# First graph layer of the last four spans by running sums over gathered rows, with those spans built first and as counts only

## What is computed

```python
x1 = x
for l in range(3):                      # GRU layers, float32
    m   = x1 @ weight[l]
    agg = segment_sum(m[src] * edge_weight[:, None], dst, 6250)
    x1  = gru_cell(agg, x1, w_ih, w_hh, b_ih, b_hh)   # r, z sigmoid; n tanh; blend
x = layernorm(x + x1)
x2 = x
for W, b in ((W0, b0), (W1, b1), (W2, b2)):           # count layers
    x2 = relu((x2 + segment_sum(x2[src], dst, 6250)) @ W.T + b)
out = layernorm(x + x2)
```

## Time and profile before

| | us |
|---|---|
| median of 3 runs | 2880.29 (2880.04 to 2880.68) |
| the profiled execution | 2883.43 |
| its span in the profile | 2881.7 |
| PE busy | 2832.6 |
| DVE, ACT, POOL busy | 1246.0, 947.4, 872.5 |
| line 1247, aggregate of the first layer, PE busy | 570.2 |
| line 1240, the build, PE busy | 346.5 |
| line 969, second and third layer, PE busy | 888.4 |
| line 1165, count layers, PE busy | 780.6 |

### The profile page before, as it was taken

The page is one execution under the profiler, slowest core; times in us unless marked ns, Lnnn a source line. Parts: engine busy times, 40 slices in busy tenths (PEclk is TensorE's granted clock), DMA queues, the critical chain, the costliest instruction groups (busy, mean ns, idle before and its releaser), DMA issues.

```text
span 2881.7 us, 72532 instructions
## 1 busy us (share of the span) xinstructions
PE 2832.6 (98%) x29387; PEld 1881.3 (65%) x29387; DVE 1246.0 (43%) x2716; ACT 947.4 (33%) x1891; POOL 872.5 (30%) x1007
## 2 busy tenths in 40 slices
PE   6999999999999999999999999999999999999998
PEld 5899999999999955555555555555655555555554
DVE  7678877777888514344422344343500010001011
ACT  6777777777777610000001011101400010001111
POOL 4344344443444315554541454544000000000000
PEclk7999999999999999999999999999999999999999
DMA  5666666666662398998996988988487868886884
GB/s 196 267 262 244 245 261 261 257 241 251 262 263 95 113 397 342 350 339 326 355 369 253 340 338 331 357 330 327 149 326 301 310 248 301 309 304 247 318 304 163
DMA packets 134009, 810.64 MB, mean 281 GB/s; under 512 B 17208, under 2 KB 27308, under 8 KB 113948
## 3 DMA queue, kind: packets, MB, share of 16 engines
q1 hardware_dynamic: 111228, 758.32, 67.9%
q0 software_dynamic: 19968, 40.46, 4.4%
q10 hardware_dynamic: 2720, 10.62, 0.9%
HBM read 553.01 MB, written 256.33 MB: 281 GB/s over the span
## 4 chain that ended last, share of the span: by engine, by line
PE 95%; issue 2%; DVE 1%; ACT 1%; DMA 1%; another core or an unknown queue 0%; POOL 0%; DVEq 0%; SPq 0%; ACTq 0%; POOLq 0%
PE ps L969 29%; PE ps L1165 27%; PE ps L1247 19%; PE ps L1240 11%; PE ps L979 1%; PE ps L980 1%; PE ps L1260 1%; PE ps L1261 1%; PE ps L982 1%; PE ps L981 1%; PE ps L1144 1%; ACT ring L1661 0%; DMA sum_rows<-ring 0%; PE ps L1266 0%; PE ps L1267 0%
## 5 line engine op out<-in xcount | busy, mean ns | idle before, releaser
L969 PE MATMUL ps<-ring,Y 128*128 128x448 f32 x2352 | 888.4, 539 | 0.0
L1165 PE MATMUL ps<-ring,Y 128*128 128x448 f16 x4116 | 780.6, 352 | 0.0
L1661 ACT ACTIVATE ring<-ps 128x490 f16<-128x490 f32 (+1 forms) x1344 | 698.3, 651 | 176.7 <-PE ps L1240 169.1
L969 PEld LDWEIGHTS ps<-ring,Y 128*128 128x128 f32 x2352 | 446.4, 190 | 434.8 <-issue 434.8
L1165 PEld LDWEIGHTS ps<-ring,Y 128*128 128x128 f16 x4116 | 402.7, 98 | 373.8
L863 POOL DMA_INDIRECT ring<-y_rows,ring x448 | 431.4, 963 | 518.9 <-PE ps L969 257.7
L1247 PE MATMUL ps<-ring,Y 128*128 (+1 forms) x2744 | 570.2, 360 | 0.4 <-ACT shared L1620 0.4
L1247 PEld LDWEIGHTS ps<-ring,Y 128*128 128x128 f32 x2744 | 503.6, 190 | 8.4 <-ACT shared L1620 0.8
L1240 PEld LDWEIGHTS ps<-shared 64*128 64x128 bf16 x18816 | 320.4, 93 | 76.6 <-issue 59.3
L1240 PE MATMUL ps<-shared 64*128 64x49 bf16 (+1 forms) x18816 | 346.5, 189 | 20.0 <-issue 9.6
L1824 DVE TENSOR_SCALAR ring<-ring 128x128 f32<-128x128 f32 x446 | 130.9, 294 | 388.7 <-DMA ring<-y_rows,ring 205.0
(11 more groups left out here) (196 smaller groups left out, 1450.6 us busy)
## 6 DMA issues: line engine op xcount, KB each, us to landing
ring<-adj_w SPq DMA_DIRECT2D x72, 2688.0 KB
ring<-adj_h SPq DMA_DIRECT2D x42, 2800.0 KB, 9.4
ring<-adj_h SPq DMA_DIRECT2D x42, 2688.0 KB, 9.2
adj_w<-ring SPq DMA_DIRECT2D x48, 2016.0 KB, 11.9
adj_h<-ring SPq DMA_DIRECT2D x56, 1372.0 KB, 5.4
ring<-adj_w SPq DMA_DIRECT2D x24, 2912.0 KB
adj_w<-ring SPq DMA_DIRECT2D x48, 728.0 KB, 6.8
sum_rows<-ring SPq DMA_DIRECT2D x62, 448.0 KB
```

The lines of the kernel that those rows point to most:

```text
L969: mm = pe.matmul(ps[:, bank, 0:GW], Y[:, h, :], slab(s)[:, :, h - h0, :], start=(h == 0), stop=(last and h == TILES - 1))
L1165: mm = pe.matmul(ps[:, par, 0:GW], part[:, h, :], counts_slab(par, s)[:, :, h - h0, :], start=(h == 0 and part is Y_high), stop=(h == TILE ...
L1661: act.activation(strip[:, :, c0:c0 + UNIT * WIN].rearrange("p h (d j) -> p d h j", d=WIN)[:, :, :, w0:w1], psum_unit(a)[:, :, kind, :, :]. ...
```

## The change

The build goes through the spans in another order, `ORDER`: the last four first, then the other 24. The last four are built as counts only: DVE makes two of the three one-hot instructions, PE does one product for each pair and node instead of three, ACT evicts each unit once, POOL makes two casts instead of seven steps, SP stores the counts alone, and no tiles of these spans are added. Their first layer is done by running sums as in the other two layers: the list of edges is loaded at the start, POOL gathers 224 rounds of rows of `x` during the build of the 20 spans in slots 5 to 24 (`RUN_SLOTS`), 11 rounds in a slot and 12 in every fourth, each placed at a half batch of its own (`ROW_POINTS`); ACT scales a round two batches after its gather and DVE adds it four batches after; SP stores four rounds at a time. Two of the rounds stand inside and ahead of `make_columns`. The ends are placed on DVE ahead of slot 25, fetched by POOL in slots 26 and 27, and the four spans' gates follow the last tiles, with `add_tiles` of the last span cut into six parts around them (`TAIL_TILES`); the gates of span 23 come last. The turns of the inputs (`TURNS`) move from batches 4 to 14 to batches 12 to 22.

In all three layers the rows are now summed in place: 16 buffers (`RUN_BUFS`) take the place of 10 and 14, a gather waits for the store of the round 16 before it, and the last two stores of the second and third layer are POOL's (`LAST_STORES`). The loops of DVE, ACT, POOL and SP over the spans are written out; PE keeps its loop. Weights and lists move to other places in SBUF, and the space for POOL's DMA descriptors is set to 8192.

```diff
-ROW_BUFS = 10
-STORE = 7
+RUN_BUFS = 16
+STORE = 4
+FIRST_RUN = GATHERS - RUN_SPANS
+ORDER = [*range(FIRST_RUN, GATHERS), *range(FIRST_RUN)]
+GATE_ORDER = [*range(FIRST_RUN - 1), *range(FIRST_RUN, GATHERS), FIRST_RUN - 1]
+RUN_SLOTS = range(RUN_SPANS + 1, GATHERS - 3)
+ROW_POINTS = [1, 2, 3, 4, 5, 7, 8, 9, 11, 12, 15]
+MORE_POINTS, MORE_EVERY = [14], 4
+LAST_STORES = 2
+SCALE_LAG, SUM_LAG, STORE_LAG = 2, 4, 5
+PLACE_SLOT, ENDS_SLOT = 25, 26
+TAIL_TILES = [0, 6, 15, 24, 33, 42, TILES]
...
+            def fetch_round(turn, i):
+                if i >= RUN_BUFS:
+                    if i % STORE == 0:
+                        use, q = divmod(i // STORE - STORE_TURNS, STORE_TURNS)
+                        pool.wait_ge(s_stored[q], stored_by(turn, q) + 16 * (use + 1))
+                    pool.wait_ge(s_acc, RUN * turn + i - RUN_BUFS + 2)
+                pool.indirect_dma_start(out=run_bufs[:, i % RUN_BUFS, :], out_offset=None, in_=y_rows if turn else x,
...
+            def fetch_at(t, points):
+                for point in points:
+                    i, (k, half) = round_at(t, point), divmod(point, 2)
+                    if i is None:
+                        continue
+                    if half:
+                        pool.wait_ge(s_bev, evicted(t, k) + 1)
+                    else:
+                        pool.wait_ge(s_bmm, UNITS * (BUFS + BATCHES * t + k))
+                    pool.sem_inc(s_mark_pool, 1)
...
+                    fetch_round(0, i)
+
+            def prepare_span(t):
+                par = t % 2
+                n = BATCHES * t
+                fetch_at(t, range(0, 4))
...
+                add_own(t + 1, 1 - par)
+                fetch_at(t, range(4, 6))
+                take_places(t + 2, par)
+                if t in (ENDS_SLOT, ENDS_SLOT + 1):
+                    first = RUN_SPANS // 2 * (t - ENDS_SLOT)
+                    fetch_ends(0, range(first, first + RUN_SPANS // 2))
+                for d, (k, later) in enumerate(zip(FETCH_AT, FETCH_AT[1:] + (6,))):
+                    pool.wait_ge(s_bmm, UNITS * (BUFS + n + k))
+                    pool.sem_inc(s_mark_pool, 1)
+                    gather(par, d)
+                    fetch_at(t, range(2 * k + 1, 2 * later))
+                make_columns(t + 1, 1 - par, t)
+                fetch_at(t, [14])
+                near_rows(t + 3, 1 - par)
+                fetch_at(t, [15])
...
                 for kind in range(2):
                     col_step(pool.tensor_copy(columns[:, par, :, kind, :, :], batches(kind).to_broadcast([P, BATCHES, BATCH, 2])))
+                fetch_at(slot, [12, 13])
                 rest = batches(2)
-                for p in range(WPARTS):
+                for p in range(WPARTS if has_weights(t) else 0):
...
+            def scale_rows(n):
+                for i in rounds_at(n):
+                    row = run_bufs[:, i % RUN_BUFS, :]
+                    act.wait_ge(s_row[i % RUN_BUFS], 16 * (i // RUN_BUFS + 1))
+                    act.activation(row, row, ACT.Copy, scale=run_edges[:, i, 1:2]).then_inc(s_prod if i else s_acc, 1)
...
+            def sum_row(turn, i):
+                done = RUN * turn + i
+                row, last = (run_bufs[:, j % RUN_BUFS, :] for j in (i, i - 1))
+                dve.wait_ge(s_acc, done)
+                dve.wait_ge(s_prod, done - turn)
+                dve.scalar_tensor_tensor(out=row, in0=last, scalar=run_edges[:, i, 2:3], in1=row,
+                                         op0=ALU.mult, op1=ALU.add).then_inc(s_acc, 1)
...
+            for c, n in enumerate(range(FIRST_RUN - 2, GATHERS)):
+                add_tiles(0, TAIL_TILES[c], TAIL_TILES[c + 1])
+                if n < GATHERS - 1:
+                    fused_gates(n)
...
+                if c < RUN_SPANS:
+                    flip_run(c)
```

## The result

| | before | after |
|---|---|---|
| median, us | 2880.53 (6 runs) | 2983.39 (2977.91 to 3021.43, 6 runs) |
| profiled execution, its span | 2883.43, 2881.7 | 2982.35, 2980.6 |

After stands to before as 1.0384 (95% interval 1.0348 to 1.042): **103 us slower**, where 2830 us was forecast.

A forecast was written before the change was run, and what follows sets the result against it. PE alone was taken to bound the steady build, busy for all 820.80 us. The terms -136.8 + 70.0 - 9 + 13.2 + 12 + 0 = -50.6 on a span of 2881.7 gave 2831.1, so 2830 us, range 2806 to 2868.

The forecast's parts named there:

- Part 5: Rows in the 20 spans: PE waits 0.6 us for columns in each, +12 us; lower end 0, upper end +116.
- Part 4: Behind the steady spans: four spans' gates 9.2 us, flips 2, placing ends 2, gathers of ends nothing; +13.2 us.
- the tail: Work behind the steady spans: four spans' gates at 9.2 us and flips at 2 us, within Part 4.
- Part 1: Steady build: four spans fewer that cost PE its full time, 4 x 34.2 = -136.8 us.
- Part 2: Four spans of counts at 17.5 us each, +70.0 us; bounds 15.5 and 25.7 us a span.
- Part 3: The start: first one-hot sooner, -3 us; no cold start in the first weighted span, -6; together -9, bounds -13 and +3.
- Part 6: Second and third layer: same rounds and pace, 0 us, between -2 and +20.
- Rival 1: Slots with rows: POOL's gathers make columns late and PE waits in each; chance 0.09 of 2886 or more, 0.05 of 2874 to 2886.
- rivals 2 to 4: 2: count spans cost 25.7 us, 2863, chance 0.08; 3: stores hold rows, 2850, 0.06; 4: all covered, 2806 or less, 0.07.

The follow-up runs named there:

- j3: Changed kernel without row gathers, scalings and additions in slots 5 to 24, with 197 counting instructions on PE that move its loop: 2828.6 us, 0.982 of before.
- j2: Changed kernel with 197 counting instructions on PE (70 at the start, 4 in each batch of counts) and nothing else: 2885.0 us, 1.0022 of before.
- j1: Changed kernel with 197 counting instructions on PE, gathers released by a building batch's first third, near gather earlier, ends one at a time: 2855.0 us, 0.9913 of before.
- e2: Changed kernel with POOL's 224 row gathers alone left out, ACT's scalings and DVE's additions kept: 2940.9 us.
- h4: Changed kernel with 198 counting instructions ahead of PE's program, ends last, near gather first, row gathers in pairs behind the end of a building batch: 2995.2 us.
- h1: Changed kernel with 198 counting instructions ahead of PE's program, moving its loop to the place it had in before: 2966.4 us.
- e4: Changed kernel with the 16 gathers of ends behind the near gather of slots 25 and 26 and the four joins last: 2925.2 us.
- e1: Changed kernel with row gathers, scalings and additions of slots 5 to 24 left out, only semaphores counted up: 2916.7 us, 1.0081 of before.

## Why the prediction was wrong

The miss up to the second layer, step by step, in the profile of after:

| step | forecast, us | measured, us | miss |
|---|---|---|---|
| not in the sum: PE's loop code lost 4 times | 0 | 4 x 13.4 | +53.6 |
| Part 5, rows in slots 7 to 24 | 18 x 0.6 | 18 x 4.1 | +62.8 |
| Part 4, slots 25 to 27 over 34.2 each, less a loss | 2 | 36.2 - 13.4 | +20.8 |
| slots 5 and 6 over 34.2 each | 1.2 | 8.3 | +7.1 |
| Parts 2, 3 and the tail, what is left | | | +3 |

**Part 1** was right: j3 has 34.20 us for every span from slot 9 on and is 51 us faster than before. **Part 2**: count spans are 19.5 us on average (58.60 / 3), not 17.5; the bounds of 15.5 and 25.7 hold them. **Part 3** took 6 us off because the first weighted span wouldn't pay a cold start, and took the spans behind it to be steady ones. But the 75.6 us of the next two spans in the earlier trace rows are 7.2 over that: PE ran on newly loaded code there (q8 has packets until 133 us, and PE is idle for 3.0 and 2.0 us until "issue"). After pays this as well, in slots 5 and 6 (76.7 us). Even so the first three parts with the tail are right to some 10 us: without rows the forecast would have been 2818, and j3 measured 2828.6.

**Part 4**: the tail came out as worked out: from the last transposes to the second layer after takes 51.5 us and before 40.7, where 11.2 more were forecast. The 16 gathers of ends were put at nothing, since they go "where POOL has 20 us free". That holds in j2 and fails in after, where they stop PE for some 20 us. **Part 6** was right: +2.2 us of -2 to +20.

**Part 5** is the step that failed by its own terms: it priced rows at 0.6 us a slot, and they cost 4.1. The sum asked only when the columns come, and that was right: in slot 19 DVE's first one-hot came 9.7 us after batch 5, which began at 693.28, where 9.5 to 11.1 had been worked out. But POOL's gathers cost in two other places. One could have been read: "nothing else on POOL is urgent", the prediction says, and the near gather is, since its landing decides when DVE counts steps. In j2, which has this wait (2.0 us a span) and no pauses, rows cost 2.7 us a span; in j1, where near goes first and the gathers are released at other points, 0.4. So the 0.6 of the sum was a good figure for another order of gathers, by luck: its wait for columns was not what cost. The other, the pauses, had no row in the trace of before, because there each gather ends ahead of the next building batch; the 1.4 us that are left of the 4.1 go with them. ACT's scaling, put at 0.3 us from DVE's, took 0.43, and e2 shows that this was covered. **Rival 1** was right in sign and wrong in place; rivals 2 to 4 didn't occur.

**The loss of PE's code** had no term and no rival. The trace of before shows q8 idle through the steady build, and that was a fact to ask about: what keeps the loop loaded, and does the change touch it? It does, by the 1850 instructions of the count spans ahead of the loop. I compared engines' work and didn't count instructions.

Not settled: why two places of the loop differ; which of the other 250 are good; why the pauses go by group of runs. That POOL's gathers cause them is argued, not shown. It rests on the overlap: all 61 such batches were slow in h4, and in h1 none of the 57 free ones from 257 to 957 us. In two of the batches shown the last pause ends 0.6 and 1.6 us after the last gather on POOL, so it may be the transfers and not POOL's issuing; no run tells them apart. The removal of the gathers was only run on chips without pauses.

## What to carry to other kernels

A loop that is the bound has a state the work doesn't show: look in the trace whether its engine loads code in steady state, and when code ahead of it grows by a few instructions, look again; 58 of them cost 4% here. Count a gather by what it lies on and by what queues behind it, not by its engine's free time: the same 224 rounds of rows cost 56 us in one order and 26 in another. And compare kernels only on one chip, with the losses of each run counted: e4 seemed to gain 58 us by an edit that gains nothing.

## What the runs showed of the hardware

- PE loads its program in packets of 16 KB, 256.3 instructions each. A loop of 1661 instructions stays loaded over all its back jumps (25 in before) or loses its code at 2 to 13 of them, by where it begins. A loss costs 13.4 us over two spans (e1), with two stops of some 3 us and a granted clock of 0.50 for 6.8 us. Spans on code that was loaded for the first time took 39.2 and 36.4 us in before and 37.1 and 39.7 in after, for 34.2 us of work.
- In 3 of 6 groups of runs PE gets some five matmuls in 0.7 us about the time of an indirect DMA of POOL's, in the others its pace doesn't change (16 spans: 625.9 us in h1, 590.3 in j2).
- A counting instruction on PE takes at least 0.1 us: 198 of them at the start moved the first transposes from 20.5 us (after) to 43.1 (h1).
- ACT scales a row of 128 columns by a factor per partition in 0.43 us (after).
